# Hyperbolic message coefficients on VectorE: per-node factors moved into table columns, the tangents asked for first, turnover work placed between dependent steps

## What is computed

```python
def expmap(u, p):
    lam = 2.0 / clip(1.0 - sum(p * p), MIN_NORM)
    n = _norm(u)
    return mobius_add(p, tanh(0.5 * lam * n) * u / n)
def logmap(y, p):
    sub = mobius_add(-p, y); n = _norm(sub)
    lam = 2.0 / clip(1.0 - sum(p * p), MIN_NORM)
    return 2.0 / lam * _artanh(n) * sub / n

ricci      = _l2_normalize(tail_emb + rel_emb)
hyper_head = expmap0(head_emb)              # tanh(n) * u / n
hyper_tail = expmap(tail_emb, hyper_head)
hyper_rel  = expmap(rel_emb, hyper_head)
res = project(mobius_add(hyper_tail, hyper_rel))
res = relu(logmap(res, hyper_head) + ricci * 1e-07)
sums.at[head].add(res)                      # then the mean over the edges of each head
```

## Time and profile before

| | before |
|---|---|
| median of three runs | 24631.85 us (24630.52 to 24632.59) |
| profiled execution | 24639.28 us, span 24637.4 us |
| granted TensorE clock, mean | 0.519 (0.50 in the passes, the 1.2 GHz level) |
| POOL busy | 16804.4 us, 68% of the span |
| PE / PEld busy | 12188.6 us (49%) / 10180.9 us (41%) |
| DVE busy | 9559.8 us (39%), 15381 instructions |
| ACT busy | 2026.5 us (8%) |
| hyperbolic passes | about 4356 to 7250 us and 7440 to 10330 us |

### The profile page before, as it was taken

The page is one execution under the profiler, slowest core; times in us unless marked ns, Lnnn a source line. Parts: engine busy times, 40 slices in busy tenths (PEclk is TensorE's granted clock), DMA queues, the critical chain, the costliest instruction groups (busy, mean ns, idle before and its releaser), DMA issues. The chain is left out here.

```text
span 24637.4 us, 207525 instructions
## 1 busy us (share of the span) xinstructions
PE 12188.6 (49%) x52285; PEld 10180.9 (41%) x52286; DVE 9559.8 (39%) x15381; ACT 2026.5 (8%) x3737; POOL 16804.4 (68%) x16828
## 2 busy tenths in 40 slices
PE   3223434677766777577773345343434334334443
PEld 1111222566655666466673335333333323333332
DVE  6555444788867888711111111211111121111112
ACT  0000001222222222200010001000000000000000
POOL 4777777777756777577736773677477757774776
PEclk5555566555555555555555555555555555555555
DMA  0000001222222222211111111111211121121112
GB/s 23 2 2 12 25 24 51 49 51 52 51 34 57 51 52 52 46 27 27 27 11 30 28 28 13 28 28 28 21 28 28 28 27 28 28 27 22 28 28 27
DMA packets 756117, 757.00 MB, mean 31 GB/s; under 512 B 442264, under 2 KB 522332, under 8 KB 735826
## 3 DMA queue, kind: packets, MB, share of 16 engines
q0 software_dynamic: 528384, 505.04, 13.2%
q1 hardware_dynamic: 227410, 248.99, 3.2%
HBM read 650.94 MB, written 102.11 MB: 31 GB/s over the span
## 5 line engine op out<-in xcount | busy, mean ns | idle before, releaser
L439 POOL DMA_INDIRECT rows<-table_lin,pay x9984 | 9419.2, 943 | 4773.4 <-issue 3000.7
L1424 DVE TENSOR_TENSOR acc<-acc,pair 128x1024 f32 x832 | 1016.1, 1221 | 10663.1 <-PE pair L661 10525.0
L661 PE MATMUL pair<-rows,onehot 128*128 128x64 f32 x19968 | 4800.1, 426 | 0.0
L661 PEld LDWEIGHTS pair<-rows,onehot 128*128 128x128 f32 x19968 | 4493.1, 332 | 520.7 <-issue 520.7
L649 PE MATMUL pair<-ones_bf,zeros_bf 1*128 1x512 bf16 x1664 | 837.8, 604 | 7625.5 <-issue 7594.4
L439 POOL DMA_INDIRECT rows<-table_hyp,pay x3328 | 3438.0, 1033 | 1319.7 <-issue 1019.8
L649 PEld LDWEIGHTS pair<-ones_bf,zeros_bf 1*128 1x128 bf16 x1664 | 109.2, 99 | 7753.3 <-issue 7753.3
L625 PE MATMUL pair<-tab,sel_t 128*128 x6656 | 1677.1, 434 | 1286.8 <-ACT head L822 447.4
L625 PEld LDWEIGHTS pair<-tab,sel_t 128*128 128x128 f32 x6656 | 1475.8, 327 | 1599.2 <-issue 1599.2
L423 POOL DMA_INDIRECT payload_src<-rows x1600 | 1556.0, 972 | 738.1 <-issue 738.1
L423 POOL DMA_INDIRECT payload_dst<-rows x1600 | 1560.4, 975 | 493.8 <-issue 486.9
(11 more groups left out here) (299 smaller groups left out, 15326.5 us busy)
## 6 DMA issues: line engine op xcount, KB each, us to landing
rows<-table_lin,pay POOLq DMA_INDIRECT x9984, 2.4
rel<-rel_rows SPq DMA_DIRECT2D x52, 1056.0 KB, 5.5
xs<-rel_rows SPq DMA_DIRECT2D x52, 1056.0 KB, 4.9
rows<-table_hyp,pay POOLq DMA_INDIRECT x3328, 2.5
rel_rows<-rel SPq DMA_DIRECT2D x26, 1056.0 KB, 4.1
rel_rows<-xs SPq DMA_DIRECT2D x26, 1056.0 KB, 4.2
payload_src<-rows POOLq DMA_INDIRECT x1600, 2.1
payload_dst<-rows POOLq DMA_INDIRECT x1600
```

The source lines that it names most:

```text
L439: pool.indirect_dma_start(out=rows[:, h, t, 0:width], out_offset=None, in_=table[:, :], in_offset=bass.IndirectOffsetOnAxis(ap=pay[:, h, t ...
L661: last = nc.tensor.matmul(sums[:, bass.ds(at, D)], onehot[:, h, t, :], mv, start=False, stop=False, skip_group_check=True)
L1424: V.tensor_tensor(flat_acc[:, at], flat_acc[:, at], ps_half[u], ALU.add)
```

## The change

- The node table becomes TW = 104 wide: beside norm, squared norm, C_A and C_PP it now holds 1/norm (C_IN), 1 - C_PP (C_OM), the clipped 1 - C_PP (C_KC) and its reciprocal (C_IO). `prepare` computes them once for each node, 9 small instructions in place of 2. The relation rows become RW = 67 wide, with the reciprocal norm. So `messages` no longer computes them for each edge (L1243, L1247, L1258 to L1261, and the copies into NN and YY are gone); it reads the columns from `head`, `rows` and `rel`.
- The arguments of Tanh are computed first and asked for before the first large sum. The answer is taken after the first half of the one-hot matrices.
- The turnover is cut into four pieces `aside[0..3]`: one-hot half 0, adding half 0, one-hot half 1, adding half 1. They stand where a `level` stood between dependent small instructions.
- After answer 2: the square root is taken of the clipped square (N2), the projected square U2 is a clip of U1 done while ACT works, and three instructions become fused ones.
- Answer 4: ACT computes Ln(1 + A1) and Ln(1 - A1) itself, with bias and scale, and DVE subtracts, in place of computing (1 + A1)/(1 - A1) on DVE (two adds, a reciprocal, a product) and one Ln. The factor 1e-7 is folded into the argument of the square root.
- `firsts`: a second small table (a DMA that is stored and loaded beside `blocks`) holds the block number clipped to NB - HG. DVE's `add_half` reads it in place of `blocks`; PE's `sum_group` loads it into one more register. This shortens the accumulator from NB + 15 to NB + 2 blocks, so its memset goes from 128x7232 to 128x6400. The type matrices' room moves to the head buffer's.

In all, DVE runs 96 instructions for a group in place of 109, and 13 drains fewer.

```diff
-TW = 100
-C_EE, C_NE, C_A, C_PP = 96, 97, 98, 99
-RW = D + 2
+TW = 104
+C_EE, C_NE, C_IN, C_A, C_PP, C_OM, C_IO, C_KC = range(96, TW)
+RW = D + 3
...
-        acc = sb("acc", [P, NB + HG - 1, D])
+        acc = sb("acc", [P, NB + 2, D])
...
                 for u in range(2):
                     sums = ps_half[u]
                     pe.load(sum_regs, blocks[0:1, bass.ds(g * G + HG * u, HG)])
-                    first = pe.snap(sum_regs[0], min_val=0, max_val=NB - 1)
+                    pe.load(first_reg, firsts[0:1, bass.ds(2 * g + u, 1)])
+                    first = pe.snap(first_reg, min_val=0, max_val=NB - HG)
...
-                    answer(g, h, 2, U1, U2, ACT.Sqrt)
+                    answer(g, h, 2, N2, N2, ACT.Sqrt)
...
-                    answer(g, h, 4, A1, A1, ACT.Ln)
+                    await_reg(act, "act", S["asked", m], 4 * g + 4)
+                    nc.scalar.activation(LN[:, 0, :], A1, ACT.Ln, bias=iota[:, 1:2], scale=1.0)
+                    nc.scalar.activation(LN[:, 1, :], A1, ACT.Ln, bias=iota[:, 1:2], scale=-1.0).then_inc(S["answered", m], 1)
...
-                V.tensor_copy(NN[:, 0, :], t_[:, :, C_NE])
-                TS(NN[:, 1, :], rl[:, :, D + 1], MIN_NORM, None, MAX)
-                V.tensor_copy(YY[:, 0, :], t_[:, :, C_EE])
-                V.tensor_copy(YY[:, 1, :], rl[:, :, D])
+                TT(T1[:, 0, :], nt, io, MUL)
+                TT(T1[:, 1, :], nr, io, MUL)
                 V.tensor_copy(Q4[:, 0, :], ss)
-                TS(OM, pp, -1.0, 1.0, MUL, ADD)
-                level()
-
-                ttl(prod, hd[:, :, 0:D], t_[:, :, 0:D], MUL)
+                TT(US, tt_, rr, ADD)
+                TT(prod, hd[:, :, 0:D], t_[:, :, 0:D], MUL)
+                ask(m)
...
-                between()
-                V.reciprocal(RN, NN)
-                TS(KC, OM, MIN_NORM, None, MAX)
-                level()
-                V.reciprocal(DC, KC)
-                level()
-                TT(T1, NN, both(DC), MUL)
-                ask(m)
-                meanwhile()
-                TT(U3, YY[:, 0, :], YY[:, 1, :], ADD)
+                aside[0]()
+
                 answered(m, g, 1)
-                ttl(BB, T1, RN, MUL)
+                TT(BB[:, 0, :], T1[:, 0, :], it, MUL)
+                TT(BB[:, 1, :], T1[:, 1, :], ir, MUL)
+                aside[1]()
                 TT(T1, BB, BB, MUL)
...
+                aside[2]()
...
+                aside[3]()
...
                 answered(m, g, 3)
-                TS(A1, SQ[:, 0, :], ARTANH_MAX, None, ALU.min)
+                TS(A1, SQ[:, 0, :], ARTANH_MAX, None, MIN)
+                ask(m)
                 V.reciprocal(RS, SQ)
-                level()
-                TS(B1, A1, -1.0, 1.0, MUL, ADD)
-                TS(U1, A1, 1.0, None, ADD)
-                level()
-                V.reciprocal(B1, B1)
-                level()
-                TT(A1, U1, B1, MUL)
-                ask(m)
-                TS(U2, RS[:, 1, :], 1e-7, None, MUL)
-                TS(U3, RS[:, 0, :], 0.5, None, MUL)
-                level()
                 answered(m, g, 4)
-                ttl(U3, U3, A1, MUL)
+                ttl(B1, LN[:, 0, :], LN[:, 1, :], SUB)
+                STT(out=U3, in0=B1, scalar=0.5, in1=RS[:, 0, :], op0=MUL, op1=MUL)
+                level()
```

More of the change, by code:

```diff
@@ L145, in build @@
         tile_off = [flat_rows.bitcast(I16)[:, 2 * (4840 + 20 * k):2 * (4840 + 20 * k) + TPP] for k in range(2)]
+        tile_first = [flat_rows.bitcast(I16)[:, 2 * (4848 + 20 * k):2 * (4848 + 20 * k) + TPP] for k in range(2)]
         tile_cmp = flat_rows[:, 4900:4900 + TPP * NB].rearrange("p (t b) -> p t b", b=NB)
@@ L1187, in _ @@
             prepare(0, squares_early)
+            for j in range(4):
+                own = slice(R * j, R * j + R)
+                ts(relblk[own, j, D + 1:D + 2], relblk[own, j, D + 1:D + 2], MIN_NORM, ALU.max)
+                recip(relblk[own, j, D + 2:D + 3], relblk[own, j, D + 1:D + 2])
             for i in range(2):
@@ L1221, in four, with messages @@
                 return v.unsqueeze(1).to_broadcast([P, 4, G])
-            def messages(m, g, h, between, meanwhile):
+            def messages(m, g, h, aside):
                 t_, hd, rl, hot_ = rows[:, h, :, :], head[h], rel[h], type_hot[:, h, :, :]
                 prod = msg[:, :, 0:D]
-                ss, aa, pp = hd[:, :, C_EE], hd[:, :, C_A], hd[:, :, C_PP]
+                ss, aa, pp, om, io, kc = (hd[:, :, c] for c in (C_EE, C_A, C_PP, C_OM, C_IO, C_KC))
+                tt_, nt, it = (t_[:, :, c] for c in (C_EE, C_NE, C_IN))
+                rr, nr, ir = (rl[:, :, D + c] for c in range(3))
                 TT, TS, STT, level = V.tensor_tensor, V.tensor_scalar, V.scalar_tensor_tensor, dve.drain
-                MUL, ADD, SUB, MAX = ALU.mult, ALU.add, ALU.subtract, ALU.max
+                MUL, ADD, SUB, MAX, MIN = ALU.mult, ALU.add, ALU.subtract, ALU.max, ALU.min
                 SH, HY, RT = Q4[:, 0:2, :], Q4[:, 1:3, :], Q4[:, 2:4, :]
                 C1, C2 = CC[:, 0:2, :], CC[:, 2:4, :]
-                c1, d1, c2, d2 = (CC[:, k, :] for k in range(4))
+                d1, d2 = CC[:, 1, :], CC[:, 3, :]
                 c12, d12 = CC[:, 0:3:2, :], CC[:, 1:4:2, :]
@@ L1351, in messages @@
                 level()
-                TS(DC, DD, 1.0, MIN_NORM, ADD, MAX)
+                V.reciprocal(DC, DC)
                 STT(out=U1, in0=DD, scalar=1.0, in1=U1, op0=ADD, op1=MUL)
@@ L1355, in messages @@
                 level()
-                V.reciprocal(DC, DC)
-                level()
                 TT(U1, U1, DC, MUL)
-                TT(KC, KC, DC, MUL)
+                TT(KD, kc, DC, MUL)
                 level()
@@ L1436, in hyp_group @@
                 await_reg(dve, "dve", rel_moved[h], 16 * i + ((m + 1) * LOADED + 16))
-                messages(m, 2 * i + h, h, between, meanwhile)
+                messages(m, 2 * i + h, h, aside)
             def run_pass(m):
```

129 lines of the change are left out of this document (73 added, 56 removed).

## The result

| | before | after |
|---|---|---|
| median | 24632.22 us (24630.52 to 24636.16, 4 runs) | 24342.98 us (24333.01 to 24370.34, 4 runs) |
| profiled execution, span | 24637.4 us | 24368.5 us |
| ratio | | 0.9884, 95% interval 0.9867 to 0.9901 |
| DVE busy, instructions | 9559.8 us, 15381 | 9424.1 us, 14053 |
| pass 0, mean of 50 intervals between multiplies | 54.61 us | 50.34 us |

The forecast was 24342. The median meets it, but the two hyperbolic passes do not look as forecast: pass 0 is faster than 51.7 us a group, and in pass 1 the groups change between some 50 and 54.5 us.

What follows compares the result with a forecast made beforehand. A closed cycle was taken to bound it: POOL's multiply holds DVE's first half, delaying additions and gathers. 280 (periods) + 14 (pass ends) + 6 (memset) - 10 (costs) = 290 us off 24631.85 gave 24342 us; range 24262 to 24490.

Steps and rivals of the forecast that it cites:

- Part D: DVE from answer 3 to the coefficients, 4.6 us: 1.0 us a group saved, with Ln asked for at once.
- part C: DVE from answer 2 to answer 3, 5.1 us: 1.16 us less work, 0.8 lost waiting for ACT, 0.4 saved.
- Part A: DVE from the start of `messages` to L1281, 23.8 us: 1.9 to 2.0 us a group saved, including four merged drains.
- The step to POOL: From the start of POOL's multiply (S) to its first gather (G): 9.1 us, not 12.2 or 11.6.
- The period: One group in the hyperbolic passes: 42.6 + 9.1 = 51.7 us, against 54.6 in pass 0.
- DVE is 4.5 early: DVE's coefficients stand 38.1 us after the first gather, while POOL's next multiply still starts 42.6 us after it.
- more than forecast: Rival, 5%: the gathers' stretch under DVE's products falls; period 50.6 to 51 us, time 24250 us.
- the first rival: DVE saves only 1.5 to 2.5 us, its first half is still caught; gain 1 to 2 us a group, 24480 us; 19%.
- The first half must end before S: DVE's first-half addition escapes being held only if over when POOL's multiply starts; forecast to end 0.85 us before.
- The costs: Node instructions between passes, larger table to store, small DMA behind GRU 1, PE's extra register load: together 10 us.
- The end of a pass: The last group of a pass, 48.8 us, shrinks by 3.4 and 3.5 us: 2 x 7 = 14 us saved.
- slower, by PE's sums: Rival, 7%: PE's extra register load in each half makes DVE wait for the second sum in the turnover; 24700 us.

Runs made afterwards that it cites:

- h1: The changed kernel with POOL's multiply also waiting until DVE has ended the first half of its addition: 24293.45 us, ratio 0.9862.
- j1: The changed kernel with two 128x32 copies and their drains added on DVE behind the fourth answer: 24507.68 us, ratio 0.9942.
- i1: The kernel before with only the fourth answer's part of the change (two logarithms on ACT, DVE subtracts): 24677.05 us, ratio 1.0001.
- g1: The changed kernel with eight 128x32 copies added on DVE behind the fourth answer: 24624.47 us, ratio 0.9995.
- f1: The changed kernel unaltered, beside the kernel before on a chip of some 32000 us: 31997.82 us beside 31855.24, ratio 1.0045.
- f2: The changed kernel with POOL's multiply also waiting for DVE's first half, on a chip of some 32000 us: ratio 1.0170.
- e and f runs: Eight runs of unaltered, added-wait, reordered-copy, extra-copy and fourth-answer-only kernels on two chips where both kernels take about 32000 us: ratios 0.9950 to 1.0225.

## Why the prediction was right, and where not

**What bounds the kernel: right.** The closed cycle of gathers, multiply, held half and late additions was read from the earlier trace rows, and h1, j1 and i1 show it: each moves the time by what it does to the held half.

**DVE's savings: right in kind, 0.9 too small.** From the large product to the coefficients DVE was to take 41.3 - 3.0 = 38.3 us and takes 37.36. Part D gave 0.92 (forecast 1.0) and part C 0.54 (0.4; the wait for answer 3 is 0.47 in the rows above). Part A was the undersized term: 2.27 from the product on, where 1.6 were forecast. Not priced was the idle time ahead of each addition to the accumulator, twice a group. Before (DVE's timeline, the group of the earlier trace rows):

```profile
5567.64 1.22 DVE L1424 TENSOR_TENSOR acc<-acc,pair 128x1024 f32 x1 [0.65 <-issue]
```

The small steps now lie in it, and 0.23 and nothing are left. How much of the 2.27 is the merged drains was not measured apart. But eight copies of 128x32, each with a drain, took 2.3 to 2.8 us in g1, 0.29 to 0.35 each, and two 0.52 in j1, where instructions without a drain between them start 0.10 apart. The rule of the Trainium skill that the prediction weighed ("VectorE: DVE Perf Modes", section "Rules for kernel authors") is not what these rows show.

**The step to POOL: right.** G was to come at S + 9.1 and came at S + 9.05. The hand-overs took 0.34 and nothing between the additions (0.3 forecast); but the additions are stretched to 4.91 by DVE's openers, and the gap ahead of the first gather is 0.15 and not 0.57 to 0.8.

**The period: wrong in both directions.** "DVE is 4.5 early" rested on gathers of 42.6 us. They now take 40.8 to 42.0 in the free groups, as the prediction's rival "more than forecast" had it: of 32 gathers the second is stretched, to 1.86 us (in some groups the last too, to 2.00), where before two near the front were, to 2.61 and 1.99 or to 3.09 and 1.97. Why the second of these two is spared, the rows do not show. So pass 0 costs 50.34 a group in place of 51.7. The same 1.3 us are taken from DVE's room: its first half began 1.0 to 2.1 us ahead of the multiply and not 2.1 (0.85 + 1.2) throughout, and in pass 1, where DVE is some 0.5 us later, 0.6 us ahead in nearly every second group. That is the condition of the first rival, at a saving that was larger than forecast, not smaller. The text took the size of the room from the old span of the gathers, although it said itself that this would change. Each rival thus held in one pass, and their mean, (50.34 + 51.94) / 2 = 51.1, stands near 51.7.

**The condition itself: too strict, and that saved the forecast.** "The first half must end before S" was taken for granted. In 38 of the first 50 groups of pass 0 it starts less than 1.23 us ahead and so is not over at S, yet it is not held; by the prediction's own condition all of them would have been. The real edge (0.68 to 0.60 us ahead) left the groups of pass 0 some 0.3 to 0.4 us on the free side, and those of pass 1 that were held less than 0.1 on the other. Had DVE saved only the 3.0 us that were forecast and not 3.94, the groups of pass 0 would by the same sum have started 0.1 ahead and been caught too (an estimate from 1.0 - 0.9). On which side a pass fell was luck.

**The signs that were named.** No wait of DVE for PE's sum in the turnover, and ACT's table load for Ln 0.32 us after answer 3 was read (5560.41 against 5560.09): as forecast. "Wrong if the additions still wait over 1 us for DVE" came true in 22 of the 52 groups of pass 1 (1.30 and 1.59 us in the rows of the held group).

**The costs: too small.** Ten microseconds were put down. The profiled execution has 12.2 ahead of pass 0 (2.6 in h1, so this varies) and 42 to 44 in pass 2. There PE adds the edge weights as well (L674) and comes last; DVE waits for it and POOL for the edge list behind DVE. PE's clearing and POOL's wait for that list in 500 us of pass 2, after and before (from the list of waits: us in total, times, longest us):

```profile
PE pair L659 <- issue: 149.1, 24, 12.1
...
POOL rows L447 <- DMA pay<-payload_src: 26.5, 12, 2.8
```
```profile
PE pair L649 <- issue: 138.1, 24, 11.7
...
POOL rows L439 <- DMA pay<-payload_src: 15.6, 11, 1.8
```

149.1 / 24 - 138.1 / 24 = 0.46 us a half, 0.92 a group, 48 in 52 groups, and POOL's wait grew by as much (10.9 us in 12 groups, 0.91 each). What changed there is the one register more that `sum_group` loads. The prediction priced it "up to 1 us" at the end of passes and weighed more of it only in the hyperbolic passes, where it is hidden: the second clearing of a group waits 0.47 us there and waited 0.17 before. It was not undone in a run of its own, so the cause is read, not shown. The Trainium skill ("Runtime: NRT & Kernel Launch", section "Instruction fetch mechanics") gives some 200 ns a register for the loads that the runtime itself puts in, which read from HBM. The load here reads SBUF and stands among matmuls; by these rows it cost PE 0.30 to 0.46.

**The end of a pass:** 14 were forecast, and 48.8 to 46.3, 49.0 to 46.0 and 2.7 between the passes make 8.

So the sum of 290 was met by a gain of 345 in the multiplies (280 + 14 forecast) less costs of 345 - 289 = 56 (10, less 6 for the memset, forecast). What bounds the kernel and what frees it was right; that two terms were 51 and 52 us too small and cancel, so that the median lies 1 us from the forecast, is luck.

**The rival "slower, by PE's sums"** was given 7%, with 1.6 us to spare. On the chip of the result PE's second sum ends at 5534.06 + 7.09 = 5541.15 and DVE wants it at 5541.51: 0.4 to spare where 1.6 were forecast, and no wait in the trace. On the other chips the wait is there, but PE's sum had ended 2.4 us (f1) and 27 us (f2) before the wait did, so it does not bear out the rival's reason.

## What to carry to other kernels

Where two engines hold each other up at one point, time against work is a step: find out on which side of the point each group lies and by how much, before adding up savings, and recompute that distance with the new length of everything in the cycle. Once the distance is small, make the order safe with a wait instead of relying on it: 0.5 us of waiting at the right place was worth more than it cost. Such a gain holds for the pace that it was measured at: on the chips of 32000 us the same wait made the kernel 1.2% slower. And an instruction added to a shared helper is priced in every stage that calls it, by what is last there.

## What the runs showed of the hardware

- A DVE addition with two SBUF inputs (128x1024, 1.23 us) that meets POOL's multiply is held until 1.1 us after its end, also when it had started up to 0.60 us ahead of it: 5.32 us. Started 0.68 us ahead it was not held in any group, and the multiply took 4.04 us in place of 3.65. Which of the two started first does not decide here. The other way round POOL's pair of additions grew from 4.35 to 4.91 us beside DVE's openers, and one of these, 32 columns wide, took 2.21 us.
- Chips of one kind differed by 30% on this kernel (the kernel before took 24632 to 24675 us beside the result, g1, h1, i1 and j1, and 31979 and 31855 beside the e and f runs), and the sign of the change with them: 0.9884 on one, 1.0045 on another. The gathers' pitch was the same on both (1.25 us); the small steps of all other engines during the gathers were not.
- PE's granted clock, 0.50 in pass 0 before, is 0.54 there after. The rows show it right behind the two sums, which PE ran from 5525.58 to 5541.15 with one gap of 0.47 us: eight head products that take 2.03 us at the 1.2 GHz level took 1.13. Before, PE stood idle for 3.7 us soon behind the same sums and stayed at that level; here it went on with hardly a gap.

```profile
5545.80 1.13 PE L634 MATMUL pair<-tab,sel_t 128*128 x8 [0.64 <-ACT xs L832]
...
5556.20 2.03 PE L634 MATMUL pair<-tab,sel_t 128*128 x8 [6.57 <-ACT xs L832]
```

It changed next to nothing: in the list of DVE's waits from 4500 to 6950 us those for the head rows sum to 3.6 us.
